# A mixture-of-experts transformer block: the front stage takes a third window of the shared expert, between the steps of the routing

## The reference

```python
def ffn(hidden, gate_w, shared_wg, shared_wu, shared_wd, exp_wg, exp_wu, exp_wd):
    xf = hidden.reshape(T, 256)                       # T = 4096 tokens
    scores = sigmoid(xf @ gate_w.T)                   # 8 experts
    topk_w, topk_idx = top_k(scores, 2)
    topk_w = 2.5 * topk_w / (topk_w.sum(-1, keepdims=True) + 1e-20)
    shared_out = silu(xf @ shared_wg.T) * (xf @ shared_wu.T) @ shared_wd.T     # 352 wide
    h = silu(einsum('td,efd->etf', xf, exp_wg)) * einsum('td,efd->etf', xf, exp_wu)   # 176 wide
    all_out = einsum('etf,edf->etd', h, exp_wd)
    routed_out = (topk_w[..., None] * picked(all_out, topk_idx)).sum(axis=1)
    return shared_out + routed_out

x = x + 0.5 * ffn(layernorm(x)); x = x + attention(layernorm(x)); x = x + 0.5 * ffn(layernorm(x))
```

## Time and profile before

| | |
|---|---|
| median of 3 runs | 1339.91 us (1338.66 to 1339.95) |
| the profiled execution's own time | 1341.68 us |
| its span | 1339.6 us |
| mean granted TensorE clock | 0.929 |
| busy share of the span: TensorE, VectorE, ScalarE, GpSimd | 87%, 73%, 59%, 40% |
| layer 1: front 18.7 to 121.3, experts to 277.4, combine to 377.3 | 102.6, 156.1, 99.9 us |
| layer 2: front 982.0 to 1085.6, experts to 1242.0, combine to 1339.6 | 103.6, 156.4, 97.6 us |

### The profile page before, as it was taken

How to read it: one execution, slowest core, us unless ns; L and a number is a source line. 1 busy time by engine, 2 the same in 40 slices (tenths; PEclk the granted TensorE clock), 3 DMA queues, 4 the chain that set the end, 5 groups by cost and what they waited for, 6 DMA issues and landing times. The chain is left out here.

```text
span 1339.6 us, 38859 instructions
## 1 busy us (share of the span) xinstructions
PE 1163.8 (87%) x13796; PEld 866.7 (65%) x13796; DVE 982.0 (73%) x2151; ACT 793.1 (59%) x1944; POOL 535.3 (40%) x738
## 2 busy tenths in 40 slices
PE   1873999989859969999998999999858659999897
PEld 1653999968748825555554555553746559999686
DVE  6666666648869879998887888893586766666586
ACT  1645666663226606877776777788636466666631
POOL 0642444337715512322332322333516334442576
PEclk9975999989969969999998999999979769999899
DMA  6320444423355651222221222210234114443354
GB/s 206 127 80 28 128 132 134 125 74 95 96 190 196 220 92 47 67 59 62 60 63 52 62 59 60 63 39 3 95 113 128 49 56 131 131 134 111 99 150 137
DMA packets 96384, 132.43 MB, mean 99 GB/s; under 512 B 15644, under 2 KB 81116, under 8 KB 96220
## 3 DMA queue, kind: packets, MB, share of 16 engines
q1 hardware_dynamic: 74716, 86.07, 21.4%
q0 software_dynamic: 13056, 35.67, 9.7%
q10 hardware_dynamic: 8448, 8.39, 1.8%
HBM read 81.35 MB, written 48.23 MB: 97 GB/s over the span
## 5 line engine op out<-in xcount | busy, mean ns | idle before, releaser
L1740 ACT ACTIVATE s_PR<-s_ps_b 128x512 f32<-128x512 f32 (+3 forms) x768 | 331.1, 496 | 123.2 <-PE s_ps_b L1851 118.1
L1760 DVE TENSOR_REDUCE s_MX<-s_ps_a 128x1 f32<-128x512 f32 (+3 forms) x608 | 357.9, 653 | 50.4 <-PE s_ps_a L1829 47.3
L1851 PE MATMUL s_ps_b<-QO,KO 99*32 99x512 bf16 (+3 forms) x3072 | 217.2, 329 | 8.1 <-issue 3.6
L1711 POOL TENSOR_SCALAR_AFFINE_SELECT s_PR<-s_PR 128x256 f32<-128x256 f32 x256 | 103.2, 406 | 301.7 <-ACT s_PR L1740 296.1
L792 POOL DMA_INDIRECT f_XG<-xn_scratch,f_tok_u x144 | 136.1, 945 | 206.2 <-PE f_ps_x L888 137.7
L1829 PE MATMUL s_ps_a<-KO,QO 96*32 96x512 bf16 (+3 forms) x3072 | 212.2, 338 | 1.4 <-DVE s_MX L1760 1.2
L1003 POOL DMA_INDIRECT f_YG<-y_scratch,f_slots_u x128 | 128.3, 1003 | 87.4 <-issue 33.8
L1868 PE MATMUL s_ps_o<-s_PR,s_VG 128*17 128x512 f32 (+3 forms) x1536 | 158.8, 488 | 1.0 <-POOL s_PR L1711 0.6
L898 PE MATMUL f_ps_u<-f_W,f_xh 128*128 x576 | 152.8, 348 | 0.0
L1851 PEld LDWEIGHTS s_ps_b<-QO,KO 99*32 99x32 bf16 x3072 | 81.3, 96 | 90.7 <-ACT s_PR L1740 44.4
L1829 PEld LDWEIGHTS s_ps_a<-KO,QO 96*32 96x32 bf16 x3072 | 81.2, 99 | 69.3 <-DVE s_MX L1760 24.6
(11 more groups left out here) (227 smaller groups left out, 2637.8 us busy)
## 6 DMA issues: line engine op xcount, KB each, us to landing
y_scratch<-f_YS SPq DMA_DIRECT2D x144, 128.0 KB, 1.7
qk_scratch<-p_QK SPq DMA_DIRECT2D x32, 384.0 KB, 3.1
QO<-qk_scratch SPq DMA_DIRECT2D x96, 128.0 KB, 2.8
KO<-qk_scratch SPq DMA_DIRECT2D x96, 128.0 KB, 2.8
xn_scratch<-f_XN ACTq DMA_DIRECT2D x16, 512.0 KB, 4.0
f_RAW<-in_w_up SPq DMA_DIRECT2D x16, 352.0 KB, 3.2
X<-in_x SPq DMA_DIRECT2D x4, 1024.0 KB, 9.4
x_scratch<-X SPq DMA_DIRECT2D x1, 4096.0 KB, 16.4
```

What stands on the lines that cost most here:

```text
L1711: nc.gpsimd.affine_select(out=tile, in_=tile, compare_op=ALU.is_ge, fill=0.0, base=0, pattern=[[0, 2], [1, P]], channel_multiplier=-1)\
L1740: nc.scalar.activation(PR[:, u // 2 % SLOTS, u % 2, 0:W - lo], ps_b[u % RING][:, lo:W], ACT.Exp, scale=SCALE).then_inc(exp_done, 1)
L1760: nc.vector.tensor_reduce(MX[:, h:h + heads, i, s], ps_a[slot][:, 0:heads * keys].rearrange("p (h n) -> p h n", h=heads), AX.X, ALU.max).t ...
L1851: last = nc.tensor.matmul(ps_b[u % RING][strip, lo:W], KO[k][0:RM, h, i * P + strip.start:i * P + strip.stop], QO[k][0:RM, h, hf * W + lo: ...
```

## The change

`FRONT` goes from 2 to 3. The front stage now does the shared expert of windows 0 to 2 (tiles 0 to 11), and the combine stage has five windows (20 tiles) in place of six. The third window's work isn't in the loop over windows; it is put between the routing's steps:

- TensorE: `down(0)`, `up(2, 0)`, `counts`, `up(2, 1)`, `down(1)`, `up(2, 2)`, the first four groups of `tokens`, `down(2)`, the last four.
- ScalarE: its silu, rounding and the weight copies of experts 6 and 7 alternate; expert 7's copies stand behind `token_ids(1)`.
- VectorE: `gated_h(2, 0)` behind the first two `add_shared`, `gated_h(2, 1)` behind `place`, `gated_h(2, 2)` behind `one_hot(1)`, `h_low_2(2)` behind `one_hot(2)`, and two more `add_shared` behind `units`.
- GpSimd: `h_low(2, 0)` and `h_low(2, 1)` between the low halves of experts 6 and 7.

The buffers of the rounded hidden rows keep two places (`w % 2`) and `h_high` of window 2 waits for `down(0)`. `RSEL` moves from `H` to `RAWS`, the counts' PSUM from `ps_u` to `ps_x`, and window 2's split halves from `XT` to a block of `W`. Two waits go (VectorE's for `hl_pool` ahead of `find`, TensorE's for `h_ready` ahead of the counts).

```diff
-        self.FRONT = 2
+        self.FRONT = 3
...
-        hs = [sb("hh", [P, NF, HC, 4 * P], F32R), sb("hl", [P, NF, HC, 4 * P], F32R)]
+        hs = [sb("hh", [P, 2, HC, 4 * P], F32R), sb("hl", [P, 2, HC, 4 * P], F32R)]
...
-        RSEL = H[:, :, :].rearrange("p b n -> p (b n)").bitcast(F16).rearrange("p (b g r) -> p b g r", b=2, g=CH)
+        RSEL = taken(RAWS, 0, CH * P).bitcast(F16).rearrange("p (b g r) -> p b g r", b=2, g=CH)
...
-        ps_count = ps_u[0][:, :].rearrange("p (k n) -> p k n", k=2)
+        ps_count = ps_x[0][:, :].rearrange("p (k n) -> p k n", k=2)
...
-            for n in range(5, E):
-                expert_low(n)
+            expert_low(5)
+            expert_low(6)
+            h_low(2, 0)
+            h_low(2, 1)
+            expert_low(7)
...
+                if w >= 2:
+                    act.wait_ge(y_done, 2 * w - 2)
...
-            for n in range(NW - 2, E):
-                expert_high(n)
+            silu(2, 0)
+            expert_high(6)
             act.wait_ge(pre_done, 1)
             nc.scalar.activation(PRE[:, :], ps_count[:, 0, :], ACT.Copy).then_inc(pre_copied, 1)
             nc.scalar.activation(TOT[:, :], ps_count[:, 1, :], ACT.Copy).then_inc(pre_copied, 1)
-            for n in range(8):
+            h_high(2, 0)
+            silu(2, 1)
+            h_high(2, 1)
+            silu(2, 2)
+            token_ids(0)
+            token_ids(1)
+            h_high(2, 2)
+            expert_high(7)
+            for n in range(2, 8):
                 token_ids(n)
...
-            dve.wait_ge(hl_pool, 2 * NF)
...
             add_shared(0)
             add_shared(1)
+            gated_h(2, 0)
             weigh()
             place()
+            gated_h(2, 1)
             slots(0)
             slots(1)
             divide()
-            for n in range(8):
+            one_hot(0)
+            one_hot(1)
+            gated_h(2, 2)
+            one_hot(2)
+            add_shared(2)
+            h_low_2(2)
+            one_hot(3)
+            add_shared(3)
+            for n in range(4, 8):
                 one_hot(n)
-                if n == 1:
-                    add_shared(2)
-                if n == 3:
-                    add_shared(3)
             units()
+            add_shared(4)
+            add_shared(5)
             dve.wait_ge(tok_done, 8)
...
-                pe.wait_ge(h_ready, HC * NF)
...
             down(0)
+            up(2, 0)
             counts()
+            up(2, 1)
             down(1)
-            for n in range(8):
+            up(2, 2)
+            for n in range(4):
+                tokens(n)
+            down(2)
+            for n in range(4, 8):
                 tokens(n)
```

More of the change, by code:

```diff
@@ L140, in front_stage @@
     NF = S.FRONT
-    assert NW == E == 8 and HC == 3 and NF == 2
+    assert NW == E == 8 and HC == 3 and NF == 3
     XBLOCK = E - NF
@@ L336, in h_low @@
                 pool.wait_ge(hh_done, HC * w + m + 1)
-                nc.gpsimd.tensor_tensor(hs[1][:, w, m, :], H[:, (HC * w + m) % 2, :],
-                                        hs[0][:, w, m, :].bitcast(F32), ALU.subtract).then_inc(hl_pool, 1)
+                nc.gpsimd.tensor_tensor(hs[1][:, w % 2, m, :], H[:, (HC * w + m) % 2, :],
+                                        hs[0][:, w % 2, m, :].bitcast(F32), ALU.subtract).then_inc(hl_pool, 1)
             expert_low(0)
@@ L392, in h_high @@
                 act.wait_ge(h_ready, n + 1)
-                nc.scalar.activation(hs[0][0:CHUNKS[m][1], w, m, :], H[0:CHUNKS[m][1], n % 2, :],
+                if w >= 2:
+                    act.wait_ge(y_done, 2 * w - 2)
+                nc.scalar.activation(hs[0][0:CHUNKS[m][1], w % 2, m, :], H[0:CHUNKS[m][1], n % 2, :],
                                      ACT.Copy).then_inc(hh_done, 1)
@@ L431, in _ @@
                     silu(*divmod(q - 2, HC))
-            h_high(NF - 1, HC - 1)
+            h_high(1, HC - 1)
             copy_logits(NW - 1)
@@ L496, in h_low_2 @@
                 dve.wait_ge(hh_done, n + 1)
-                nc.vector.tensor_tensor(hs[1][0:used, w, 2, :], H[0:used, n % 2, :], hs[0][0:used, w, 2, :].bitcast(F32),
+                nc.vector.tensor_tensor(hs[1][0:used, w % 2, 2, :], H[0:used, n % 2, :], hs[0][0:used, w % 2, 2, :].bitcast(F32),
                                         ALU.subtract).then_inc(hl_dve, 1)
@@ L698, in down @@
                             used = CHUNKS[m][1]
-                            last = nc.tensor.matmul(ps_y[pair][:, i * D:(i + 1) * D], hs[a][0:used, w, m, at:at + P],
+                            last = nc.tensor.matmul(ps_y[pair][:, i * D:(i + 1) * D], hs[a][0:used, w % 2, m, at:at + P],
                                                     WS[b][0:used, m, :], start=n == 0, stop=n == len(plan) - 1)
```

## The result

The changed kernel takes 1357.97 us (median of four runs, 1355.81 to 1358.97), the kernel before 1339.93 (1338.66 to 1340.70): ratio 1.0131, 95% interval 1.0115 to 1.0147. It is 18.0 us slower where +10.1 was forecast, and 2 us outside the wider range (1342 to 1356). The sign was right, and the combine stage and the tables came out within 1 us a layer of their terms. What failed is the term "front, up to the tables": it took VectorE's operand to be ready in time, and it was not. Attention, which the sum put at nothing, adds 2.1 us in the profiled pair.

A forecast was written before the change was run, and what follows sets the result against it. VectorE and ScalarE were taken to bound the tables, VectorE the routing, TensorE and GpSimd's fetches together the combine stage. Front +16.0 and combine -5.9 make +10.1 us, so 1350.0; likeliest range 1346 to 1354, wider 1342 to 1356.

The forecast's parts named there:

- front, up to the tables: Routing chain before the tables: removed blocking, new work and blocking elsewhere nearly cancel, -0.1 us a layer (-2.9 to +1).
- Attention: Stage whose code is unchanged: the forecast's sum has no term for it, 0 us.
- The combine: Combine stage with one window less: GpSimd's fetches limit the saving to 5.1 us in layer 1, 0.8 in layer 2.
- The tables: End of the front stage: inserted third-window work lengthens it by 8.1 us a layer.
- the stall before step 6: Tables: VectorE stands still 4.5 us until TensorE finishes group 4, which comes behind `down(2)`.
- old blocking: Routing chain: GpSimd's slowing of VectorE's selection steps goes away, -4.2 us a layer.
- new work: Routing chain: VectorE's added `gated_h` steps cost +1.3 us a layer.
- other blocking: Routing chain: GpSimd slows VectorE's weighing, scan and slots instead, +3.0 us a layer.
- (a): Tables: same mechanism, but `down(2)` runs at the full clock in both layers, giving 1346.0 us; chance 0.16.
- (b): Combine stage: follows TensorE alone, so the last fetch comes 13.5 us earlier, giving 1328.9 us; chance 0.06.
- (c): Front stage: hides the new work without a stall, -0.2 us a layer, giving 1333.6 us; chance 0.08.
- (d): Front stage: `down(2)` wholly at low clock, blocking at upper bounds, +10.9 us a layer, 1356.7 us; chance 0.06.

The follow-up runs named there:

- the front alone: Changed kernel's three-window front stage, but combine stage still six windows (tiles 8 to 11 get the shared expert twice): 1394.06 us (1.0141) in a slow session, rerun 1356.72 (1.0130).
- the combine alone: Kernel before with five combine windows, front stage unchanged (tiles 8 to 11 without the shared expert): 1360.38 us (0.9895) in a slow session, rerun 1333.20 (0.9944).
- the run with memsets: Changed kernel with GpSimd writing zeros in place of its subtractions in the routing (low halves of experts 6 and 7, window 2's remainders): 1349.45 us (1.0070).

## Why the forecast was right, and where it failed

**The combine** (forecast -5.1 and -0.8). Right in the sum: -4.5 and -1.9 up to VectorE's end, at an unchanged 0.95 + 0.30 us for each fetch. Layer 2 gave more than its upper bound of 1.3; of its 1.9, GpSimd's busy time gives 1.4 (65.06 to 63.64 us), which is the longer single fetches. The barrier then took 2 us in layer 1. The step said that the stage ends 3.2 us and three VectorE steps behind the last fetch's start; it ends 7.05 us behind it, for GpSimd, which no row before could show, since GpSimd was never last.

**The tables** (forecast +8.1). Measured +7.1 in both layers. `down(2)` at the low clock and the stall before step 6 are as worked out; blocking was 1.6 us, not 2.5, and fell on steps 4 and 5; the stall was 3.2 us, not 4.5.

**Front, up to the tables** (forecast -0.1; its own parts add up to +0.1). This is the term that failed: +3.2 in layer 1, +2.1 in layer 2, beyond its upper bound of +1. By its parts: -4.2 of old blocking, right; +1.3 of new work, right; other blocking 4.2 us, not 3.0; and 1.9 us of waiting in layer 1, 0.8 in layer 2, which the sum did not have. The step that was wrong is the one that let TensorE run `down(0)` at the full clock and so had `up(2, 0)` ready before VectorE asked. It rests on the granted 1.00 of the earlier trace rows, which is layer 1's. Layer 2 of the same trace has the same products at 0.50 for their first 4.2 us:

```profile
core 0: us, PE busy (x), PEclk, DMA share, GB/s
1046.70:1050.90 4.20, 4.20 (x20) 0.50 0.25 83
```

In the profiled execution after, the clock rose only at about 86.4 us. Where `down(0)` did run at the full clock, in layer 2 of the second run of the front alone, `gated_h(2, 0)` did not wait, L552 took 0.46 us and not 1.12, and the chain took 20.53 us, +0.6 on the kernel before:

```profile
1057.12 0.68 DVE L503 TENSOR_TENSOR f_H<-f_H,f_ps_u 128x512 f32<-128x512 f32 x1
1057.72 0.46 DVE L552 TENSOR_TENSOR f_DEN<-f_M 128x32 f32<-128x32 f32 x1
```

Layer 1 of the first such run agrees (no wait, 20.55). In the layers of the other traces that keep the change's order of steps and GpSimd's subtractions, the wait is 0.75 to 1.93 us and the chain 22.0 to 23.2, longer with the wait. So the late operand costs its own wait and 0.7 us of blocking behind it. Over two layers the term was 5.5 us short.

**Attention** (forecast 0). +2.1 us in the profiled pair; over all traces 614.0 us is the mean of the six with the long pause and 609.4 that of the eleven with a short one, +4.6. The forecast put it at nothing since its code is unchanged; what moved is the place of its loop in TensorE's program, 19 instructions earlier.

**The sum.** In the span: 10.1, +5.5 for the chain, -2.0 for the tables, +1.4 for the combine, +2.1 for attention, -2.4 for loops and experts, makes 14.7 against 14.5 measured. The medians are 18.0 apart, 3.5 more, since the profiled execution before lay 1.8 us above its median and that of after 2.2 below; in which stage an average execution loses them was not resolved. Without the long pause the change costs 13.05 us by the medians (1352.03 - 1338.98) and 14.2 by the ratio (1.0106).

**The rivals.** (a), `down(2)` at the full clock, did not happen in either layer. (b), the combine following TensorE, was refuted by the run of the combine alone. (c), the front hiding the work, is out at +19.4 us of routing. (d) came near in size, 1356.7, but for other reasons: it had `down(2)` wholly at the low clock.

## What to carry to other kernels

When two engines bound a stage together, halve the one that keeps its load before you count on relieving the other: with half the fetches the window was worth 8 to 10.5 us, with all of them 2 to 4.5. Work put into a chain in which each step waits for the last must have its operand ready by the worst clock seen for its producer, not the best (`down(0)` began at 1.00 in one layer and at 0.50 in the other), so read the producer's row in every layer of the trace; else move a step that needs nothing (here the weigh) ahead of it, and cut long TensorE work into pieces between the ones that others wait for. And after an edit look for waits that the profile puts down to "issue" in stages that you did not touch: here TensorE's loop of 5034 instructions stood still for 3.25 to 7.38 us at its jump, by how many instructions the edit had left ahead of it, and when it was written out ScalarE stood still at the same place for 2.74 and 3.73 us.

## What the hardware showed that was not expected

- At TensorE's jump back in a loop of 5034 instructions TensorE stood still for 3.25 to 4.76 us in eleven traces and for 6.58 to 7.38 in six. Three instructions more ahead of it took the pause from 7.27 to 3.98 us, 236 more from 3.62 to 6.58. Written out, a stop of ScalarE of 2.74 or 3.73 us showed at the same place.
- In layer 1 of the changed kernel attention began 7.05 us after the start of GpSimd's last indirect fetch, and GpSimd's first instruction behind the barrier 7.02 us after it, though the rows had landed at 2.70 and VectorE was done at 4.19. The nine other traces with all 64 fetches and five windows have 7.05 or 7.06 at the same place. In layer 2 the rows landed at 3.45 us and were used at 3.47.
- A VectorE step that took 0.18 us in the run with memsets (L553) took 2.61 us beside GpSimd's subtractions: three of them ran in that time, and it ended 0.04 us behind the last, while the step before it took 1.12 us and ended behind the first border (L552).
- `down(0)` ran at a granted clock of 1.00 from its start in one layer of the kernel before (82.4 to 87.0 us) and at 0.50 for its first 4.2 us in the other (from 1046.7), with the same code.
- In one session the same kernel took 1376.67 us where it took 1339 to 1340 in the others; with half the fetches it took 1339.76 there. It is not a trait of the chip: the next session, recorded under the same chip number, gave 1339.18.
